# Fused tokens, attention and experts on one core: attention stacks transposed by the DMA engine, routing moved within the head, weights in pieces, second convolution in front

## What is computed

```
h = tok(x)                    # conv 8x8 patches -> 128, 2 layers of linear attention + MLP, head to 192
h = concat([h, txt])          # 1536 tokens
h = h + attn(layernorm(h))    # 12 heads of 16; the queries are the keys as well
      q = (h @ Wq.T + bq), plain reshape to (12, 1536, 16)    # so "head" n is token tile n: 128 tokens x 12 groups
      q = q / max(|q|, 1e-12);  v = (h @ Wv.T + bv) as (1536, 12, 16)
      sim = -(AA - 2 AB + AA^T) * 16**-0.5;  out = softmax(sim) @ v
h = h + ffn(layernorm(h))     # rmsnorm, gate, top 4 of 16 experts, swiglu MLP 192 -> 2x384 -> 192, weighted sum
```

## Time and profile before

| | |
|---|---|
| median of 3 runs (lowest, highest) | 745.86 us (744.64, 749.47) |
| the profiled execution: its own time, its span | 744.08 us, 742.3 us |
| PE, DVE, ACT, POOL busy over the span | 87%, 61%, 51%, 47% |
| mean granted TensorE clock | 0.949 |

### The profile page before, as it was taken

How to read it: one execution, slowest core, us unless ns; L and a number is a source line. 1 busy time by engine, 2 the same in 40 slices (tenths; PEclk the granted TensorE clock), 3 DMA queues, 4 the chain that set the end, 5 groups by cost and what they waited for, 6 DMA issues and landing times.

```text
span 742.3 us, 17563 instructions
## 1 busy us (share of the span) xinstructions
PE 646.7 (87%) x5070; PEld 430.3 (58%) x5071; DVE 450.2 (61%) x1478; ACT 380.0 (51%) x721; POOL 350.4 (47%) x401
## 2 busy tenths in 40 slices
PE   5888899888883999999999999549999999999970
PEld 5776786678651222222222222338999999999960
DVE  0345857675665267777777763446776676767660
ACT  0323337433312799999999999203443444444330
POOL 3111323132332045555555544422778777777781
PEclk9999999999997899999999999759999999999995
DMA  8999999300021992000000000048988998888844
GB/s 331 405 347 300 338 334 319 136 1 1 12 64 53 381 318 101 30 30 30 30 30 30 31 31 33 30 163 265 255 238 232 248 252 231 233 257 235 227 63 76
DMA packets 46064, 124.74 MB, mean 168 GB/s; under 512 B 5243, under 2 KB 31292, under 8 KB 44748
## 3 DMA queue, kind: packets, MB, share of 16 engines
q1 hardware_dynamic: 32780, 108.92, 44.5%
q0 software_dynamic: 11696, 14.19, 9.8%
q10 hardware_dynamic: 1552, 1.18, 0.5%
HBM read 105.53 MB, written 58.42 MB: 221 GB/s over the span
## 4 chain that ended last, share of the span: by engine, by line
PE 59%; DVE 11%; DMA 11%; POOL 7%; issue 5%; ACT 4%; SPq 1%; DVEq 0%; ACTq 0%; POOLq 0%
PE ps L843 14%; PE ps L830 10%; PE ps L982 7%; DMA out<-mid 5%; PE ps L1011 5%; PE ps L992 4%; PE ps L684 3%; DMA odd_sum<-mid 3%; ACT mid L1104 2%; POOL rstd L467 2%; POOL mid L590 2%; DVE stat L1192 2%; DVE mid L1200 2%; PE ps L760 1%; PE ps L657 1%
## 5 line engine op out<-in xcount | busy, mean ns | idle before, releaser
L1104 ACT ACTIVATE mid<-ps 128x1536 f32<-128x1536 f32 x144 | 200.2, 1458 | 29.4 <-PE ps L830 29.4
L843 PE MATMUL ps<-mid 128*32 128x384 f32 x1152 | 123.9, 502 | 1.3
L982 PE MATMUL ps<-mid,big 128*128 128x128 f32 x756 | 99.2, 282 | 0.3 <-ACT mid L1130 0.3
L1534 DVE TENSOR_SCALAR mid<-ps,big 128x128 f32<-128x128 f32 x189 | 54.6, 345 | 69.2 <-PE ps L992 51.9
L982 PEld LDWEIGHTS ps<-mid,big 128*128 128x128 f32 x756 | 91.9, 194 | 4.3 <-ACT mid L1130 0.5
L590 POOL TENSOR_TENSOR mid<-mid 128x384 f32<-128x384 f32 x63 | 68.5, 1087 | 54.1 <-DVE mid L1543 33.5
L830 PE MATMUL ps<-mid 52*128 52x512 f16 x432 | 87.4, 386 | 5.5 <-ACT mid L1104 4.9
L1137 ACT ACTIVATE mid<-mid 128x384 f32<-128x384 f32 x63 | 32.9, 522 | 85.4 <-DVE mid L1534 84.1
L1011 PE MATMUL ps<-big,mid 128*128 x378 | 69.2, 330 | 3.2 <-POOL mid L590 2.9
L541 POOL DMA_INDIRECT expert_in<-big,slot_u x48 | 47.9, 998 | 46.5 <-DVE slot_u L1425 35.5
L1011 PEld LDWEIGHTS ps<-big,mid 128*128 128x128 f32 x378 | 60.4, 190 | 6.3 <-issue 6.2
(11 more groups left out here) (224 smaller groups left out, 1089.8 us busy)
## 6 DMA issues: line engine op xcount, KB each, us to landing
big<-w_cat SPq DMA_DIRECT2D x63, 576.0 KB, 4.0
expert_in<-expert_in SPq DMA_DIRECT2D x16, 1774.5 KB, 48.7
big<-expert_in SPq DMA_DIRECT2D x63, 136.5 KB, 3.6
big<-patches SPq DMA_DIRECT2D x3, 2048.0 KB, 20.5
w_cat<-w_a SPq DMA_DIRECT2D x1, 6144.0 KB, 32.8
big<-w SPq DMA_DIRECT2D x1, 4608.0 KB, 14.6
w_cat<-w_b SPq DMA_DIRECT2D x2, 1536.0 KB, 31.0
big<-patches SPq DMA_DIRECT2D x4, 512.0 KB, 7.4
```

Source lines behind the costliest of these rows:

```text
L843: last = nc.tensor.matmul(oacc[32 * g:32 * g + 32, 0:QW], vhead[par][:, kb, :], probs[kb % 3][:, g * QW:(g + 1) * QW], start=(kb == 0), st ...
L982: last = nc.tensor.matmul(banks[half][:, c * P:(c + 1) * P], w1_t[q][:, half * FF + c * P:half * FF + (c + 1) * P], xtT[r][:, 0:P], start= ...
L1104: nc.scalar.activation(probs[kb % 3], SETS[kb % 2], ACT.Exp, scale=0.5).then_inc(probs_ready, 1)
L1534: last = nc.vector.tensor_scalar(glu[r][:, c * P:(c + 1) * P], bank(1 + r)[:, c * P:(c + 1) * P], b1_cols[:, bass.ds(ex * 6 + c, 1)], 7.0, ...
```

## The change

1. The slots of `schedule()` are the same, but its second and third entries change places: `conv` of image 1 now stands ahead of `T` of image 0. Image 1's patches come in four pieces like image 0's, and its two token tiles are computed side by side.
2. The stacks are transposed by two DMA transposes a head from SP's queue (12 blocks of 128x128 for the keys, 8 for the queries) instead of PE and DVE. `key_tok` has each head's 52 numbers twice, 64 apart, and `qry_more` repeats two blocks for the third group of queries: three copies more at the end of `prep`, while the six of `stack_copy` go. The token rows lie in `big` instead of `mid`. SP issues a head's transposes after `stack_ready` and, from n = 2, after all scores of head n-2; PE waits for `stack_in` before the next head's first scores, and `prep` before it overwrites the rows.
3. The weights' transfers are cut into eight pieces, one behind the transposes of each of the stacks 2 to 9.
4. The routing steps are put after kb = 1, 6, 7, 9 instead of 1, 7, 8, 10.

```diff
+    order[1:3] = [order[2], order[1]]
...
+            def stacks(n, par):
+                sp.wait_ge(stack_ready, n + 1)
+                if n >= 2:
+                    sp.wait_ge(scores_ready, (n - 1) * KEYB)
+                sp.dma_start_transpose(out=keysT[par].rearrange("c (h n) -> c h n", n=P), in_=key_flat).then_inc(stack_in, 16)
+                sp.dma_start_transpose(out=qrysT[par][:, 0:8 * P].rearrange("c (j n) -> c j n", n=P),
+                                       in_=qry_flat).then_inc(stack_in, 16)
...
+                if stage == "S2":
+                    sp.wait_ge(acc_taken, weights_read)
+                    stacks(0, 0)
...
-            sp.wait_ge(vhead_ready, 1)
-            sp.dma_start(w2_sb, w2).then_inc(w_in, 16)
-            sp.dma_start(cat[:, :, 0:768], w1_a.rearrange("p (e c) -> p e c", e=E)).then_inc(w1_joined, 16)
...
-            sp.wait_ge(tr_taken, tr_base(NT - 2))
             sp.dma_start(b2_sb, b2).then_inc(b2_in, 16)
...
+            sp.wait_ge(acc_taken, TOK_ACC)
+            for n in range(1, NT):
+                stacks(n, n % 2)
+                if 2 <= n < 2 + len(pieces):
+                    dst, src, s = pieces[n - 2]
+                    sp.dma_start(dst, src).then_inc(s, 16)
...
-                if stage == "conv" and b == 0:
+                if stage == "conv" and b < 2:
...
-                if stage == "S2":
-                    pe.wait_ge(trk_taken, trks)
-                    pe.wait_ge(ctxw_taken, ctxws)
-                    for g in range(2):
-                        stacks(g, 0, g)
...
                         if kb + 2 == KEYB:
-                            pe.wait_ge(tr_taken, base + (2 if first else 3))
+                            pe.wait_ge(stack_in, n * 32 + 64)
...
-                        if kb == 2: stacks(0, n + 1, base + 1)
-                        if kb == 5: stacks(1, n + 1, base + 2)
-                        if kb == 7: t_transpose(r, 1 - par, base + 3)
-                        if kb == 8: logits(base + 4)
-                        if kb == 10: ranks(r, base + 5)
+                        if kb == 6: t_transpose(r, 1 - par, base + 1)
+                        if kb == 7: logits(base + 2)
+                        if kb == 9: ranks(r, base + 3)
...
+                if not isinstance(n, int) or n:
+                    dve.wait_ge(stack_in, n * 32)
...
-                nc.vector.tensor_copy(pairs(qry_tok[:, :, 50:52]), halves(key_tok[:, :, 48:50])).then_inc(stack_ready, 1)
+                nc.vector.tensor_copy(key_both[:, :, 1, 0:50], key_tok[:, :, 0:50])
+                step(nc.vector.tensor_copy(pairs(qry_tok[:, :, 50:52]), halves(key_tok[:, :, 48:50])))
+                nc.vector.tensor_copy(qry_more[:, :, 0:STK], qry_late).then_inc(stack_ready, 1)
```

More of the change, by code:

```diff
@@ L71, in schedule @@
     lanes += [(b, LANE if b else FIRST_LANE, b, (3 * b, 3 * b + 1)) for b in range(NB)]
-    return [(*lane[slot - start], b, tiles) for slot in range(len(LANE) + NB - 1)
-            for start, lane, b, tiles in lanes if 0 <= slot - start < len(lane)]
+    order = [(*lane[slot - start], b, tiles) for slot in range(len(LANE) + NB - 1)
+             for start, lane, b, tiles in lanes if 0 <= slot - start < len(lane)]
+    order[1:3] = [order[2], order[1]]
+    return order
 NORMS = ("conv", "C", "D2", "H", "N")
@@ L647, in _ @@
             b7 = bank(7)
-            b7h = bank(7).bitcast(f16)
-            def stacks(g, n, job):
-                if not isinstance(job, int) or job:
-                    pe.wait_ge(tr_taken, job)
-                if g == 0:
-                    pe.wait_ge(stack_ready, n + 1)
-                for s in range(6):
-                    last = nc.tensor.transpose(b7h[:, s * P:(s + 1) * P], stack_pair[g][:, s, :], ident16[:])
-                last.then_inc(tr_ready, 1)
             pe.wait_ge(consts_ready, NCONST)
@@ L678, in _ @@
                                 last.then_inc(acc_ready, 1)
-                if stage == "conv" and b:
+                if stage == "conv" and b >= 2:
                     pe.wait_ge(patch_in[b], 16)
@@ L879, in pe_head @@
             def pe_head(n, r, par, first, last):
-                base = 2 if first else tr_base(r)
+                base = None if first else tr_base(r)
                 for kb in range(KEYB):
@@ L912, in _ @@
             pe.wait_ge(b1_in, 16)
[L913 removed]
+            pe.wait_ge(trk_taken, trks)
+            pe.wait_ge(ctxw_taken, ctxws)
+            nc.tensor.transpose(b7[:, 0:E * 6], b1_rows, ident[0:E * 6, 0:E * 6]).then_inc(tr_ready, 1)
             pe_head(0, None, 0, True, False)
@@ L1345, in _ @@
                 if stage == "S1":
-                    dve.wait_ge(consts_ready, NCONST + 4)
+                    dve.wait_ge(consts_ready, NCONST + 5)
                     prep(0)
                     prep_squares(1)
-                if stage == "S2":
-                    for g in range(3):
-                        stack_copy(g, 0, (0, 0, 1)[g])
             prep(1)
@@ L1438, in dve_head @@
             def dve_head(n, r, par, first, last, prep2=True):
-                base = 2 if first else tr_base(r)
+                base = None if first else tr_base(r)
                 if not first:
                     output(r, base)
-                if first:
-                    for g in range(3):
-                        stack_copy(g, 1 - par, base + (0, 0, 1)[g])
-                elif not last:
-                    stack_copy(0, 1 - par, base + 1)
-                    norm_stats(r, 1 - par)
-                    stack_copy(1, 1 - par, base + 1)
-                    norm_square(r, 1 - par)
-                    stack_copy(2, 1 - par, base + 2)
-                    norm_rows(r, 1 - par)
-                    if prep2:
-                        prep_squares(n + 2)
-                    tT_copy(base + 3)
-                    choose(r, base + 4)
-                    weigh(r)
-                    place(r, 1 - par, base + 5)
-                else:
                     norm_stats(r, 1 - par)
@@ L1461, in dve_head @@
                     norm_rows(r, 1 - par)
+                if not last and prep2:
+                    prep_squares(n + 2)
+                if not first:
                     tT_copy(base + 1)
```

102 lines of the change are left out of this document (42 added, 60 removed).

## The result

The changed kernel took 743.44 us (median of 20 runs, 740.11 to 748.63) beside 747.55 us of the kernel before (20 runs, 744.54 to 752.24): ratio 0.9946, 95% interval 0.9926 to 0.9965, some 4 us faster where 13.4 were forecast. The profiled execution took 741.48 us (span 739.6) against 744.08 (span 742.3).

What follows compares the result with a forecast made beforehand. PE was taken to bound a head, ACT close behind. Token stage start -1.7, its end -1.0, attention -9.4 and tail -1.3 sum to -13.4 us, from 744.08 to 730.7, stated as 731; range 725 to 743.

Steps and rivals of the forecast that it cites:

- What bounds a head: Attention: PE is the longer engine, 18.05 us a head after the change, with ACT close behind at 16.9 us.
- so the whole 0.88 us comes off the period: Attention: stacks off PE save 0.88 us a head, 8.8 us over heads 1 to 10.
- `t_transpose` finds its input 0.7 us early. No cost, but little slack: Routing one key tile earlier: its chain sums to 17.3 us against the new period of 18.05.
- The transposes stay hidden: Attention: a head's two DMA transposes take 6 us within a window of 12.3 us and cost nothing.
- Rival (a): DMA transposes too slow, PE waits at kb = 10; 780 us at the 16 us upper bound; chance 0.12.
- Rival (b): Scatters land later, some 6 us, so `t_transpose` holds PE 0.7 to 1 us in most heads; 739 us; chance 0.18.
- Rival (c): Transposes as quick as plain transfers and PE keeps its clock at the token stage's end; 727 us; chance 0.05 below 726.
- Token stage, start: Convolution 1 ahead of `T` brings `A` and `T` of image 1 earlier: -1.7 us, from -0.6 to -2.5.
- Token stage, end: Last `PP` products and SP's last values come earlier, the values at 234: -1.0 us, between -2.1 and +10.
- Head 0: First attention head: stacks off PE save 0.6 us, since part of them lies in slack at its end.
- Tail: Behind the last head: scatters start from `ranks` one key tile earlier, moving everything up to the plan by -1.3 us.

Runs made afterwards that it cites:

- no pieces: Changed kernel with stacks waiting for the four scatters of the last routed tile, and all expert weights sent before the second head instead of in pieces: 769.22 us.
- the convolution alone: Kernel before with only the second convolution put ahead of the first `T` and image 1's patches in four pieces: 742.16 us, ratio 0.9941.
- b0: A trace of the kernel before, unchanged, in which the convolution of image 1 took 9.76 us.
- the second group: One series: changed kernel unchanged 730.07 us, with stacks waiting for scatters 729.19, with out-transposes one key tile later 742.43, with an already reached wait 730.22.
- the first experiment: Changed kernel with SP waiting, from the fourth head's stacks on, for the last routed tile's four scatters before the DMA transposes: 731.18 us, ratio 0.9786.
- the repeats: Kernels run again unchanged in later series; the changed kernel took 730.07, 731.2 and 745.67 us.
- the first four: Changed kernel with stacks waiting for scatters 731.18 us, without scatters 727.43, with out-transposes one key tile later 742.7; kernel before with only the convolution order changed 742.16.
- the next four: Changed kernel with out-transposes and routing one key tile later 742.42 us, only routing later 743.32, that plus stacks waiting for scatters 734.07, that wait without weight pieces 769.22.

## Why the prediction was right or wrong

The time, 731, was that of two series out of three in which the changed kernel was timed anew; the recorded result, 743.44, lies just outside the range. Point by point:

- **What bounds a head** (PE, with ACT close behind): right where no signal is late. There the period is 18.04 us against 18.05 forecast, in every head, and eleven steps gain 206.14 - 197.31 = 8.83 us (8.8 forecast, for heads 1 to 10).
- **The failed step** is "so the whole 0.88 us comes off the period", the term 10 x 0.88 = 8.8 us, and with it "`t_transpose` finds its input 0.7 us early. No cost, but little slack". Both take for granted that every handover from PE to ACT and DVE is as quick as in the one profiled execution of before. In the recorded execution PE's signals were up to 2.5 us late; in a head PE waited 0.96 us for ACT and 0.67 us at `t_transpose`, and the eleven steps grew by 210.92 - 206.14 = 4.8 us instead of shrinking by 8.8. The trace of before has no late signal, that of the changed kernel has them from the second head on. The kernel before has them in other series too, and there they cost it 2.4 us where they cost the changed one 13.6 to 14.8. It had 0.22 + 0.26 + 0.21 = 0.69 us of idle time of ACT in each head to take the delay up; the change removed it. That is not all of the difference: the kernel before has its signals 1.65 us late at most, the changed one 2.5, and only the changed one loses time at `t_transpose`. How much each of these is worth was not measured apart. No rival of the prediction has late signals in it.
- **The transposes stay hidden:** right. They land 4.2 and 4.7 us after their issues, the second issued 1.55 us behind the first, so both within some 6.2 us, against a window of 12.3; the 6 us of the estimate was good. The DMA engines' share in the stretch from 320 to 350 us rose from 0.10 to 0.52 without harm in the series without late signals. The weight pieces are the condition for that (no pieces: +28.8 us once). Of the two statements of the Trainium skill, the 1309 ns of "VectorE: DVE Perf Modes", The three transpose paths, can't be multiplied by the blocks: 12 and 8 blocks landed in 4.2 and 4.7 us, not 15.7 and 10.5. The full rate of "Advanced Engine Details and Errata", X-Bar Transpose (TRN2), isn't borne out at this size either: 640 KB in 6.2 us, from the first issue to the last landing, are some 103 KB/us, where plain weight rows move 316 KB/us.
- **Rival (a)** fell with that.
- **Rival (b)** named one place where time was lost (PE held at `t_transpose`, 0.67 us, near its 0.7 to 1), but not the reason. It took a late landing of the scatters; what is late is the signal of PE's out-transposes, and PE loses 0.96 us more waiting for ACT, which got its scores late. The slack was also smaller than stated: moving the out-transposes 1.34 us cost 1.15 us a head, so some 0.2 us were free and not 0.7. From the addition to `h_res` to a finished `t_row` a head takes 395.13 - 389.54 = 5.6 us (first trace of the second group), not the 5.07 us of the last head.
- **Rival (c)** did not come: in all twenty traces PE's granted clock falls to 1.2 GHz at the end of the token stage.
- **Token stage, start:** right in sign, mis-sized. Forecast -1.7; the first write of values comes at 193.0 us (mean of four traces of the changed kernel and one of the convolution alone) against 196.8 (three of the kernel before, one of them b0 with its slow convolution of image 1 at 198.4), -3.8 (-3.1 without b0). The working had the order of `T` and `A` right: `A` starts at 27.52 and 27.18 in two traces (forecast 26.8), `T` of image 1 at 32.4 to 32.8 (forecast 32.1). Of the missing 2.1 us 1.6 are image 3's convolution, 7.31 us at full clock against 8.88, which the sum had left as it was.
- **Token stage, end:** right. Forecast -1.0. In both kernels PE waits at the end for `b1_rows` (L913 before, L908 after), which stands behind the last values on SP's queue. From the first write of values to there it is 44.4 us in four traces of the changed kernel (44.0 to 44.8) and 45.4 in three of before (44.8 to 45.8): -0.9. SP's last values went out at 229.21 to 230.9 and not at 234, since the first write is 3.8 us earlier already and a transpose holds the queue for 1.3 to 2.1 us only.
- **Head 0:** forecast -0.6, not seen in the mean. From that product to the first copy of the sums it is 19.7 us in four traces (18.4 to 20.5) against 19.3 in three (19.2 to 19.5). The spread goes with the granted clock. It is full again 4.9 to 5.5 us behind that product in the three traces of before, and 5.0, 7.6, 9.3 and 9.7 us behind in the four of the changed kernel, whose head 0 then takes 18.4, 19.6, 20.3 and 20.5 us. With the clock back alike, 18.4 stands against 19.3: the saving is there, and the later return of the clock takes it back. The stretch from 240 to 246 us of the changed kernel in the recorded trace and in the first of the second group, in the columns of the earlier trace rows:

```profile
240.00:246.00 6.00, 6.00 (x45) 1.11 (x44) 3.39 (x16) 5.12 (x4) 0.44 (x1) 0.87 0.11 24
```

```profile
240.00:246.00 6.00, 6.00 (x32) 0.78 (x25) 2.82 (x14) 4.09 (x3) 2.17 (x1) 0.50 0.67 66
```

- **Tail:** right. From the last copy of the sums to the last copy of `combT` it is 18.33 us before and 16.96 after, -1.37 (forecast -1.3).
- **Sum without late signals:** -3.8 for the start, -0.6 from there to the first copy of the sums, -8.8 and -1.4 are -14.6; measured -15.3 and -13.1 in the two series. That it is so near the forecast of -13.4 is luck in part: 2.1 us too little for the start stand against 1.0 us too much for head 0.

## What to carry to other kernels

A gap that a change closes may be what absorbs part of the delays you can't see in one trace: price the change once with each handover from engine to engine a microsecond or two late, and see whether slack is left. Before an edit gets the credit for a recovered time, run the unchanged kernel beside it; here a wait that did nothing seemed worth 12 us. Of the kernels tried, the one with the stacks behind the scatters and the routing at key tiles 7, 8 and 10 is the one to keep: 734.07 us with late signals (one run, in a series in which the changed kernel itself did not run; two kernels beside it took 742.42 and 743.32) and 730.54 without, against 743 to 746 and 730 to 731 of the changed kernel.

## What the runs showed of the hardware

- PE's semaphore signals can be up to 2.5 us behind the work in stretches in which POOL issues scatters, and are then delivered in a burst (four within 0.20 us). The traces come from seven series: in three of them every trace had this (all with scatters), in the other four none. None was late in the head before the first scatter. The delay was at most 1.65 us in the kernel before, which has no DMA transposes, 2.0 us with the transposes behind the scatters (no pieces), and 2.5 us with DMA transposes beside them.
- By what mechanism it comes stays open. The experiments before the repeats all ran on the chip with number 0 of the record, the first four (three above and the convolution alone) with nothing late and the next four, nine minutes on, all late; the later series ran on 7 and 11 (nothing late) and 10 (late). So, if the number stands for one piece of hardware, it is not a fixed property of a chip. That instructions are fetched just then was not seen: the recorded trace has no packet of an instruction queue from 288 to 419 us, and late signals in each head there.
- It can be read off a trace: a consumer that starts long after its producer's end with the releaser "remote", two engines released within 0.05 us by different products, and few recorded completions of the scatters.
- A DMA transpose of 128 x 1536 or 128 x 1024 float16 lands in 3.2 to 5.5 us (in the recorded trace 4.2 and 4.7 us in most heads, in the first experiment, behind the scatters, 3.8 and 3.4) and holds the issuing queue for 1.3 to 2.2 us; behind 13.8 MB of other transfers it held it for 12.4 us.
- PE's granted clock is at 1.2 GHz at the end of the token stage in all twenty traces, and comes back to 2.4 GHz between 241.6 and 248.3 us. Between executions of the changed kernel this makes the head 0 of the attention 18.4 to 20.5 us long (from `b1_rows` to the first copy of the sums).
